# Moving the first loads and the last tile of a two-layer network on one core

## The reference

```
xn = layernorm(x)                                   # x: (4, 256, 512)
x = x + L0_attn(xn) + L0_ffn(xn)
xn = layernorm(x)
x = x + xn @ (mask*weight).T + bias + L1_ffn(xn)    # L1_ffn: low rank, silu(gate)*up

L0_ffn: g, u = xn @ (gate_t*gate_s).T, xn @ (up_t*up_s).T   # ternary int32 codes (1792, 512)
        (silu(g) * u) @ (down_t*down_s).T
L0_attn: h = xn @ Win.T + bin                       # width 64
         4 times: h += sconv(silu(ln(h))) * scl     # a scan over the 256 tokens of a sequence
                  h += silu(ln(h) @ W1.T + b1) @ W2.T + b2   # 64 -> 256 -> 64
         ln(h) @ Wout.T + bout
L1_ffn: P = xn @ U1; H = P @ V1 + b1; Z = (silu(H[:1376]) * H[1376:]) @ U2; Z @ V2 + b2
```

## Time and profile before

| | before |
|---|---|
| median of three runs | 274.27 us |
| profiled execution | 274.41 us, span 271.6 us |
| PE busy | 262.9 us, 97% of the span |
| DVE, POOL, ACT busy | 188.1, 148.4, 129.3 us |
| granted TensorE clock | 0.998 of full speed |
| read, written in memory | 20.46 MB, 2.10 MB |

### The profile page before, as it was taken

The page is one execution under the profiler, slowest core; times in us unless marked ns, Lnnn a source line. Parts: engine busy times, 40 slices in busy tenths (PEclk is TensorE's granted clock), DMA queues, the critical chain, the costliest instruction groups (busy, mean ns, idle before and its releaser), DMA issues.

```text
span 271.6 us, 4677 instructions
## 1 busy us (share of the span) xinstructions
PE 262.9 (97%) x1678; PEld 136.9 (50%) x1678; DVE 188.1 (69%) x299; ACT 129.3 (48%) x222; POOL 148.4 (55%) x182
## 2 busy tenths in 40 slices
PE   7599999999999999999999999999999999999994
PEld 2395455555545555555454554564444445444441
DVE  4688878968865888686888678888568595533314
ACT  2524487736455246574767451450176412356500
POOL 5987945396731172628456563414189990066920
PEclk9999999999999999999999999999999999999999
DMA  6999997101020010300120203100200002200004
GB/s 196 275 287 244 255 207 125 40 2 31 7 80 1 2 39 0 80 0 0 40 80 17 68 1 118 39 0 2 61 18 0 0 4 77 80 0 0 0 0 154
DMA packets 12037, 17.86 MB, mean 66 GB/s; under 512 B 880, under 2 KB 6768, under 8 KB 12016
## 3 DMA queue, kind: packets, MB, share of 16 engines
q1 hardware_dynamic: 6624, 12.23, 14.0%
q0 software_dynamic: 4960, 4.98, 11.5%
q10 hardware_dynamic: 432, 0.38, 0.4%
HBM read 20.46 MB, written 2.10 MB: 83 GB/s over the span
## 4 chain that ended last, share of the span: by engine, by line
PE 92%; DMA 3%; DVE 1%; ACT 1%; SPq 1%; issue 0%; DVEq 0%
PE bank L745 18%; PE bank L629 18%; PE bank L628 18%; PE bank L596 9%; PE bank L598 9%; PE bank L597 9%; DMA stage<-in_gate 3%; PE bank L676 3%; PE bank L590 2%; PE bank L707 2%; PE bank L697 1%; PE bank L696 1%; PE bank L665 1%; DVE X L1181 1%; PE bank L684 1%; PE bank L718 1%
## 5 line engine op out<-in xcount | busy, mean ns | idle before, releaser
L1302 POOL TENSOR_TENSOR hidl<-hid,hidh 128x512 f16<-128x512 f32 x28 | 33.0, 1178 | 31.3 <-ACT hidh L811 31.1
L628 PE MATMUL bank<-xh,gatew 128*128 128x512 f16 (+1 forms) x136 | 43.8, 341 | 2.2 <-ACT gatew L852 2.2
L628 PE MATMUL bank<-xh,upw 128*128 128x512 f16 (+1 forms) x136 | 43.9, 341 | 0.0
L629 PE MATMUL bank<-xl,upw 128*128 128x512 f16 (+1 forms) x136 | 43.8, 341 | 0.0
L629 PE MATMUL bank<-xl,gatew 128*128 128x512 f16 (+1 forms) x136 | 43.8, 341 | 0.0
L745 PE MATMUL bank<-downw,hidh 128*128 128x512 f16 x112 | 42.5, 379 | 0.0
L745 PE MATMUL bank<-downw,hidl 128*128 128x512 f16 x112 | 42.4, 379 | 0.0
L1206 POOL TENSOR_TENSOR root<-var,powers 128x4 f32<-128x4 f32 (+1 forms) x25 | 23.8, 956 | 31.8 <-DVE var L1048 31.2
L1308 POOL TENSOR_TENSOR actl<-hid,acth 128x512 f16<-128x512 f32 (+1 forms) x22 | 25.5, 1165 | 25.8 <-ACT acth L818 25.4
L906 ACT ACTIVATE silu<-bank,early 128x512 f32<-128x512 f32 x28 | 19.3, 688 | 27.4 <-PE bank L629 26.6
L1169 DVE SCALAR_TENSOR_TENSOR hid<-bank,early,silu 128x512 f32<-128x512 f32 (+1 forms) x22 | 16.5, 750 | 18.3 <-ACT silu L921 15.6
(11 more groups left out here) (183 smaller groups left out, 563.0 us busy)
## 6 DMA issues: line engine op xcount, KB each, us to landing
X<-in_x SPq DMA_DIRECT2D x7, 256.0 KB, 11.9
downw<-in_down POOLq DMA_DIRECT2D x2, 896.0 KB, 19.0
out_x<-X SPq DMA_DIRECT2D x7, 256.0 KB, 2.0
stage<-in_v SPq DMA_DIRECT2D x6, 256.0 KB, 2.7
gatew<-in_gate POOLq DMA_DIRECT2D x1, 1024.0 KB, 15.0
upw<-in_up POOLq DMA_DIRECT2D x1, 1024.0 KB, 19.5
stage<-in_mask SPq DMA_DIRECT2D x4, 256.0 KB, 2.7
stage<-in_weight SPq DMA_DIRECT2D x4, 256.0 KB, 3.0
```

Of the source, the lines that this page charges most:

```text
L628: pe.matmul(bank_of(key)[:, c], w, xh[b][:, k, c], start=(k == 0), stop=False)
L629: mm = pe.matmul(bank_of(key)[:, c], w, xl[b][:, k, c], start=False, stop=(k == KT - 1))
L1302: pool.tensor_tensor(hidl[:, n % FT, :], hid[:, n % UNITS, :], hidh[:, n % FT, :], ALU.subtract).then_inc(hid_lo, 1)
```

## The change

The number of staged code stripes goes from four to six (f = 0, 1, 2 of gate and up) and `stage` from five slots to seven. POOL's four code loads start at f = 3, and they move in the list: before, POOL issued one of 4 stripes of up ahead of everything else and one of gate behind the first root; now it issues gate's behind the second root and up's behind the fourth. The prologue has another order, with `fill` 3 and 5 in place of 5. The last token tile is computed in two halves of 256 columns in two banks, after the three other outs of its block; `zcopy` comes ahead of `attn, 1, 2`. All tables of places have new numbers.

```diff
-FIRST_LOADS = 4
-NSTAGE = 5
+FIRST_LOADS = 6
+NSTAGE = 7
...
-    dense += [("attn", 1, 1), ("hidden_end", 1), ("attn", 1, 2), ("zcopy", 1), ("attn", 1, 3)]
-    dense += [("out", 1, t) for t in range(TPB)]
+    dense += [("attn", 1, 1), ("hidden_end", 1), ("zcopy", 1), ("attn", 1, 2)]
+    dense += [("out", 1, t) for t in range(TPB - 1)] + [("attn", 1, TPB - 1), ("out", 1, TPB - 1)]
...
-PROLOGUE = (("xt", 0), ("load", 1), ("seed", 0), ("stats", 0), ("root", 0), ("load", 0), ("stats", 1), ("stats", 2),
-            ("fill", 5), ("root", 1), ("codes", "up", 1), ("norm", 0), ("root", 2), ("norm", 1), ("seed", 1),
-            ("stats", 3), ("codes", "gate", 1), ("codes", "gate", 0), ("root", 3), ("xl", 0), ("norm", 2), ("xt", 1),
-            ("first", 0, 1), ("offset", 3), ("norm", 3), ("xt", 2), ("xt", 3), ("first", 1, 1), ("first", 2, 1),
-            ("first", 0, 0), ("first", 1, 0), ("seed", 2), ("xl", 1), ("grow", 0), ("codes", "up", 0), ("grow", 1),
-            ("grow", 2), ("first", 3, 1), ("xl", 2), ("first", 2, 0), ("first", 3, 0), ("xl", 3), ("grow", 3))
+PROLOGUE = (("seed", 0), ("stats", 0), ("stats", 1), ("codes", "up", 0), ("root", 0), ("xt", 0), ("root", 1), ("load",
+            0), ("stats", 2), ("codes", "up", 1), ("seed", 1), ("norm", 0), ("norm", 1), ("fill", 3), ("stats", 3),
+            ("root", 2), ("root", 3), ("codes", "gate", 1), ("xt", 1), ("load", 1), ("codes", "gate", 0), ("xl", 0),
+            ("norm", 2), ("offset", 3), ("norm", 3), ("fill", 5), ("first", 0, 1), ("xt", 2), ("first", 0, 0), ("seed", 2), ("xl",
+            1), ("grow", 0), ("xl", 2), ("grow", 1), ("xt", 3), ("codes", "gate", 2), ("codes", "up", 2), ("first", 1, 1), ("grow", 2), ("grow", 3), ("first",
+            1, 0), ("xl", 3), ("first", 2, 0), ("first", 3, 0), ("first", 2, 1), ("first", 3, 1))
...
-CODE_LOADS = (("gate", 2, 6), ("up", 2, 6), ("gate", 6, 14), ("up", 6, 14), ("down", 0, 7), ("down", 7, 14))
+CODE_LOADS = (("gate", 3, 7), ("up", 3, 7), ("gate", 7, 14), ("up", 7, 14), ("down", 0, 7), ("down", 7, 14))
...
-LN_AT = (1.9, 2.8, 3.3, 4.2, 6.4, 10.4, 10.8, 12.3, 13)
+LN_AT = (0, 0, 0, 0, 0, 1.5, 2.3, 2.3, 6.7)
...
+            if step == ("attn", NBLK - 1, TPB - 1):
+                take(("tail",))
...
+        def halves(key):
+
+            if key == ("attn", NBLK - 1, TPB - 1):
+                return [(key, slice(0, D // 2)), (("tail",), slice(D // 2, D))]
+            return [(key, slice(0, D))]
...
-            for t in range(NTOK // P):
+            for t in range(NTOK // P - 1):
                 sp.wait_ge(out_ready, t + 1)
...
+            sp.wait_ge(last_ready, 1)
+            sp.dma_start(out[NTOK // P - 1][:, 0:D // 2], X[:, NTOK // P - 1, 0:D // 2]).then_inc(out_done, 16)
...
-                    wait_full(dve, ("attn", b, t))
-                    emit(dve.tensor_tensor(X[:, n, :], X[:, n, :], bank_of(("attn", b, t))[:],
-                                           ALU.add), out_ready)
+                    for key, c in halves(("attn", b, t)):
+                        wait_full(dve, key)
+                        emit(dve.tensor_tensor(X[:, n, c], X[:, n, c], bank_of(key)[:, c], ALU.add),
+                             last_ready if n == NTOK // P - 1 else out_ready)
```

More of the change, by code:

```diff
@@ L203 @@
[L203 to L214, removed]
+LOAD_AT = (0, 0.1, 2.7, 19.3)
+GROW_AT = (0, 0, 0.1, 0.4, 0.8, 0.8)
+LN_AT = (0, 0, 0, 0, 0, 1.5, 2.3, 2.3, 6.7)
+TABLE_AT = (5.1, 10.5, 12, 48)
+XT_AT = (7.9, 9.1, 9.3, 10.5)
@@ new lines @@
+PREP_AT = (0, 0, 2.6, 3)
+W1_AT = (16.9, 32.7)
+W2_AT = (14,)
+WOUT_AT = (20.5,)
+XBIAS_AT = (14.9, 55.9)
+MASK_AT = (29.9, 44, 52, 53.8, 64.2)
+U1_CAST_AT = (20.5,)
+V1_AT = (60.2, 62.9, 69.9, 71.4, 77.9, 88.4)
+U2_AT = (71.9, 78.8, 95.8)
+CHAIN_AT = ((8.6, 10.2, 11.8, 11.8, 13.1, 13.1, 14.1, 16.7, 17.8, 18.8, 19.7, 20.1, 22.7, 23, 25.6, 26.3, 27.1, 27.1, 29.4, 30.5, 31.8, 32.4, 33, 34.2, 37.8, 38.4, 40.6, 40.8, 41, 41, 44.5, 45.7, 47.1, 47.3, 49.5, 50, 52.4, 53.5, 55.3, 56, 57.2, 58.8, 59.6, 61.8, 63.2, 64.7, 65.4, 66.2, 68.5, 69.5, 71.7, 72, 73.3, 74.6), (13.4, 15.1, 17.7, 19, 20.9, 22.2, 24.8, 25, 27.2, 28, 30.6, 30.8, 32.5, 33.2, 34.5, 34.5, 35.1, 37.2, 38.3, 38.8, 40, 40.2, 42, 44.1, 46.1, 47.9, 49.1, 49.3, 50.5, 50.9, 52.7, 55.2, 56.1, 56.8, 58.2, 59.2, 62.5, 63.2, 64.6, 64.8, 65.5, 65.6, 68.3, 70.4, 71.7, 72.7, 73.5, 73.5, 76.7, 78.3, 81.7, 81.7, 84.2, 84.7))
@@ L217, in place_psum @@
+WMASK_AT = (72, 79, 79, 80.7)
+W_AT = (87.7, 87.7, 87.7, 92.3)
+LN1_AT = ((73.4, 73.4, 75.9, 76.1, 76.1, 76.1, 76.1, 77.7, 78.4, 80.9, 83.9, 83.9, 83.9), (90.9, 97.4, 98.9, 99.2, 100, 100, 100, 100.2, 100.2, 102.5, 103.1, 103.9, 106))
+YBIAS_AT = ((108.5, 110, 110.1, 110.1), (111.7, 113.6, 129.6, 129.6))
+V2_AT = (94.2,)
 def place_psum(order):
@@ L431, in two_layers @@
         out_ready, out_done, last_done, x0_in = sem("out_ready"), sem("out_done"), sem("last_done"), sem("x0_in")
+        last_ready = sem("last_ready")
         down_read = sem("down_read")
@@ L575, in _ @@
             sp.dma_start(bias, rows[2:4].partition_broadcast(P)).then_inc(bias_in, 16)
-            for t in range(NTOK // P):
+            for t in range(NTOK // P - 1):
                 sp.wait_ge(out_ready, t + 1)
-                c = slice(0, D // 2) if t == NTOK // P - 1 else slice(0, D)
-                sp.dma_start(out[t][:, c], X[:, t, c]).then_inc(out_done, 16)
+                sp.dma_start(out[t], X[:, t, :]).then_inc(out_done, 16)
+            sp.wait_ge(last_ready, 1)
+            sp.dma_start(out[NTOK // P - 1][:, 0:D // 2], X[:, NTOK // P - 1, 0:D // 2]).then_inc(out_done, 16)
             sp.wait_ge(out_done, 16 * (NTOK // P))
@@ L790, in _ @@
                     c = slice(t * P, (t + 1) * P)
-                    for k in range(KT):
-                        three_passes(bank_of(step)[:], [yh[b][:, k, c], yl[b][:, k, c]],
-                                     [Wh[:, k, :], Wl[:, k, :]], k == 0, False)
+                    if b * TPB + t == NTOK // P - 1:
+                        wait_bank(pe, ("tail",))
+                    for key, n in halves(step):
+                        for k in range(KT):
+                            three_passes(bank_of(key)[:, n], [yh[b][:, k, c], yl[b][:, k, c]],
+                                         [Wh[:, k, n], Wl[:, k, n]], k == 0, False)
                 elif kind == "out":
@@ L798, in _ @@
                     c = slice(t * P, (t + 1) * P)
-                    key = ("attn", b, t)
-                    three_passes(bank_of(key)[:], [zh[:, c], zl[:, c]], split["V2"],
-                                 False, True).then_inc(full_of(key), 1)
+                    for key, n in halves(("attn", b, t)):
+                        three_passes(bank_of(key)[:, n], [zh[:, c], zl[:, c]], [w[:, n] for w in split["V2"]],
+                                     False, True).then_inc(full_of(key), 1)
         @block.scalar
@@ L931, in _ @@
             last = NTOK // P - 1
-            act.wait_ge(out_ready, last + 1)
+            act.wait_ge(last_ready, 2)
             act.dma_start(out[last][:, D // 2:D], X[:, last, D // 2:D]).then_inc(last_done, 16)
```

7 lines of the change are left out of this document (removed).

## The result

The changed kernel takes 275.42 us (median of 8 runs, 274.50 to 275.80), the kernel before 274.16 us (8 runs on the same chip). The ratio is 1.004, 95% interval 1.0022 to 1.0058: slower by 0.4%, or 1.1 us, where 273.0 us was forecast. The profiled execution took 275.55 us with a span of 273.4. Outside its span lie 2.15 us, and outside that of before 2.81: the spans differ by 1.8 us and the times by 1.1, so what follows accounts for the spans.

The account below looks back on a forecast made before the run. TensorE, busy 262.9 of 271.6 us, was taken as the bound: start of useful matmuls, fixed stream, tail. Start -1.3, first hid +0.4, tail -0.35 gave -1.25 on 274.41, so 273.0 us, range 272.1 to 275.0.

Parts of the forecast that it names:

- the middle: Same matmuls after the start, small steps at new places: cost taken as 0, bounds 0 and 1 us.
- the first hid: TensorE's wait at up 3 for the bank freed by VectorE's first hid, behind tile 7: 0.4 us, bounds 0 and 3.7.
- The start: Useful matmuls begin at 10.4 us for 12.02, the 512-column stream at 19.1 for 20.41: 1.3 us gained.
- The tail: After the last matmul: the half tile's add ends 0.65 us behind TensorE, not 1.0; 0.35 us gained.
- The gap of 0.35 before the third transpose: In the start, TensorE idles 0.35 us because POOL's wide pz row delays the third tile's root and norm.
- POOL's loads out of the way: Until POOL's later-issued load 0 takes effect, at about 9.7 us, q1 and q10 have the DMA engines alone.
- The split: Sharing of DMA engine time between q1 and POOL's loads before tile 7 lands: a half for each.
- The pair named as the closest, near 98 us: Block 1, layer 1: z product and t3 transposes, 3.0 us between them for 3.46; a wait of 0.46 us at most.
- The sum: Start -1.3, first hid +0.4, tail -0.35: -1.25 us on the profiled 274.41, giving 273.0 us.
- The rival of small waits in the middle: New places, untested gaps: two or three waits of 0.5 us, 274.1 us; chance 0.12.
- The rival of a packet for a packet: Engines alternate q1 and q0 packets, q0 gets 57%, tile 7 lands at 20.0, stall 1.9, 274.5 us; chance 0.12.
- The signs that were to show the forecast wrong: Start staying at 12, a stall over 1.3 us, or waits in the middle adding up to more than 0.5.

Follow-up runs that it names:

- e9: Kernel before with the new start alone, but POOL's first two code loads at their old places, gate's first: 275.60 us, ratio 1.0042 to the kernel before.
- e12: Changed kernel with POOL's load of down's first half moved from behind the first hidl to ahead of it: 272.38 us, ratio 0.9929 to the kernel before.
- e2: Kernel before with the new tail alone (zcopy earlier, three outs ahead of the last attn, last tile in halves): 273.36 us, ratio 0.9967.
- e4: Changed kernel with the first decay table moved back on VectorE, behind hid 3 (place 7.6 for 5.1): 275.49 us, ratio 1.0039 to the kernel before.
- e6: Changed kernel with the row constants behind the first hid and the projection's constants behind the second: 276.27 us, ratio 1.0066 to the kernel before.
- e7: Changed kernel with both the first decay table on POOL and the row constants behind the first hid: 272.62 us, ratio 0.9931 to the kernel before.
- e5: Changed kernel with the first decay table made by POOL at place 9.1 instead of by VectorE at 5.1: 274.09 us, ratio 0.9984 to the kernel before.

## Why the prediction was wrong

The step that failed is the middle, which was put at 0; the stall at the first hid was also mis-sized. Start and tail came as forecast or better.

- **The start**, -1.3: right in the sum, -1.41, with errors inside that cancel. The first matmul came at 10.96 for 10.4, waiting for xl. The second norm of VectorE began later (7.72, behind POOL's second root) and took 0.92 us where 0.55 were taken; it ran beside POOL's DMA issue (rows in the last section). From the first matmul to the stream are 8.04 us, not 8.39 + 0.35. The gap of 0.35 before the third transpose did not come, since the late start hid it. And the 8.39 of before held a wait that the prediction took for work: the two transposed tiles of the third row took 1.24 us, with some 0.35 between them for ScalarE's XN, and 0.44 each in the changed kernel. So TensorE did wait between 12.1 and 268 us for more than the 0.2 of the earlier trace rows, and 0.35 us of the gain is this wait.
- **POOL's loads out of the way**: right, by e9.
- **The first hid**, +0.4: the mechanism was right, the size was not. Tile 7 landed at 19.66, not 18.5, and the stall is 1.45, outside the forecast's 0 to 0.9. The split was not the error. From 9.7 to 19.7 us q1 moved 865 packets with 1.72 MB and q0 919 with 0.92 MB, a packet for a packet, and their packets took 57.1% and 55.1% of the engines' time, a half each. What was mis-sized is q1's cost: 57.1% of 160 engine-us (16 engines, 10 us) for 1.72 MB are 53 per MB (106 ns a packet) beside POOL's loads, where 45 (82 ns) were taken from all of the first 20 us. POOL's first load landed at 19.8 in place of 16.3, the second at 22.3 for 22.9. VectorE's row constants and hid behind tile 7 took 5.90 us for 6.15 counted.
- **The middle, cost 0**: this is the step that failed. It looked at the gaps of the chain and asked whether a step's place leaves time for the steps between, by the trace of before. The first decay table is not in it: the new places put it ahead of hid 3, and beside a run of hidl on POOL. The three products took 0.58, 0.41 and 0.42 us before, and 1.42, 3.36 and 0.42 here, and TensorE waited 1.70 us at gate 5 and 0.64 for lno, 2.34 in all, outside the bound of 0 to 1. In e12 the table stands at the same place of VectorE's list and takes 0.43, 0.42 and 0.42, and both waits are gone: it is not the place by itself but what runs beside it. The pair named as the closest, near 98 us, showed no wait.
- **The tail**, -0.35: low. 0.66 in the profiles, 0.61 in e2's trace, 0.92 in its time. The last add ended 0.69 behind TensorE for 0.65 forecast; the rest is the last DMA, 2.2 us behind it for 2.5 before, the gain that was bounded by 0.3 and taken as 0.
- **The sum**: -1.25 forecast; with what was measured, -1.41 + 1.45 + 2.34 - 0.66 = +1.7 of span.

The rival of small waits in the middle had the kind of loss and not the size: it allowed for 274.1 us, and named no cause. The rival of a packet for a packet had the alternation of the queues right and the stall too high (1.9 for 1.45). The signs that were to show the forecast wrong (a stall over 1.3 us, more than 0.5 us of waits in the middle) both came, but the second before 45 us, in a stretch where only up 3 had been looked at.

## What to carry to other kernels

A move of small steps has two costs: when they end, and what runs beside them. Before a VectorE op on two SBUF operands is moved, list what POOL does at the new place; beside a run of long POOL ops it can take several times its own duration. It is safe where it ends before the run begins (e12); a DMA issue of POOL ahead of such a run is no sure place, as the changed kernel and e4 show. And of two waits one behind the other, taking the first away brings nothing while the second still stands: e6 alone would have suggested that the row constants do not matter, and e7 against e5 (0.9931 and 0.9984) shows that they do. Two waits that merge into a longer one can even cost more, when the granted clock falls behind it.
